# A gated attention and 4-bit FFN block: the order of the rotary step over ScalarE, VectorE and GpSimd

## The reference

```python
def apply_rope(x):
    phase = jnp.tile(pos[:, None] * inv_freq[None, :], (1, 2))[None, :, None, :]
    return (x * jnp.cos(phase) + rotate_half(x) * jnp.sin(phase)).astype(x.dtype)

q = (query @ Wq).reshape(b, t, 32, 128)          # query = layernorm(x)
k = (key @ Wk).reshape(b, t, 8, 128)             # key = value = ctx
v = (value @ Wv).reshape(b, t, 8, 128)
q, k = apply_rope(q), apply_rope(k)
logits = 30 * tanh(einsum(q, k) * 0.0884 / 30)
weights = softmax(where(mask, logits, -1e30))
x = x + tanh(g_xattn) * (einsum(weights, v) @ Wo)
x = x + tanh(g_ffn) * ffn(layernorm(x))          # 4-bit weights, 1376 hidden columns, SiLU
```

## Time and profile before

| what | before |
|---|---|
| median of 3 runs (lowest to highest) | 865.17 us (864.29 to 866.2) |
| the profiled execution, its own time | 864.27 us |
| its span | 862.5 us |
| mean granted TensorE clock in the span | 0.966 |
| PE busy | 774.4 us (90%), 3650 matmuls |
| DVE busy | 641.0 us (74%), 1168 instructions |
| ACT busy | 423.7 us (49%), 823 instructions |
| POOL busy | 602.7 us (70%), 437 instructions |
| chain that ended last, by engine | POOL 51%, PE 25%, issue 15%, DVE 6% |

### The profile page before, as it was taken

How to read it: one execution, slowest core, us unless ns; L and a number is a source line. 1 busy time by engine, 2 the same in 40 slices (tenths; PEclk the granted TensorE clock), 3 DMA queues, 4 the chain that set the end, 5 groups by cost and what they waited for, 6 DMA issues and landing times.

```text
span 862.5 us, 11913 instructions
## 1 busy us (share of the span) xinstructions
PE 774.4 (90%) x3650; PEld 622.0 (72%) x3650; DVE 641.0 (74%) x1168; ACT 423.7 (49%) x823; POOL 602.7 (70%) x437
## 2 busy tenths in 40 slices
PE   4757999999999999999999999999767779999998
PEld 3645777777777777777777777777655557888786
DVE  6338887888888788788878878877776668778531
ACT  2355555555555555555555555554444335555420
POOL 4567787788788778878878887879855446666510
PEclk9878999999999999999999999999887979999999
DMA  8401000300200020020002002110020024443010
GB/s 295 158 0 51 0 25 1 98 1 25 98 1 26 1 98 1 25 98 1 25 1 98 1 25 87 37 44 1 0 59 1 0 61 110 105 101 75 1 62 36
DMA packets 57137, 41.70 MB, mean 48 GB/s; under 512 B 22938, under 2 KB 44442, under 8 KB 57082
## 3 DMA queue, kind: packets, MB, share of 16 engines
q1 hardware_dynamic: 57082, 41.03, 16.2%
HBM read 38.90 MB, written 2.11 MB: 48 GB/s over the span
## 4 chain that ended last, share of the span: by engine, by line
POOL 51%; PE 25%; issue 15%; DVE 6%; ACT 1%; DMA 1%; POOLq 0%; SPq 0%; ACTq 0%; DVEq 0%
POOL aT_lo L559 10%; POOL q_rot L477 9%; POOL q_sin L472 9%; POOL probs L543 8%; POOL wo_lo L463 6%; POOL wq_lo L454 5%; PE bank_q L1146 2%; POOL wkv_lo L459 2%; PE bank_q L1147 2%; PE ps_o L52 2%; PE ps_o L54 2%; PE ps_o L53 2%; PE ps_s L52 1%; PE ps_s L53 1%; PE bank_kv L52 1%
## 5 line engine op out<-in xcount | busy, mean ns | idle before, releaser
L472 POOL TENSOR_TENSOR q_sin<-q_sin,q_tab 128x512 f32<-128x512 f32 x64 | 82.9, 1295 | 112.7 <-ACT q_sin L634 112.7
L52 PE MATMUL bank_q<-xT_hi,wq_hi 128*128 128x512 f32 x256 | 110.0, 430 | 6.2 <-ACT q_sin L634 4.8
L633 ACT COPY q_sin<-bank_q 64x512 f32<-64x512 f32 x64 | 37.3, 583 | 149.7 <-DVE q_cos L847 149.7
L52 PE MATMUL ps_o<-wo_hi,aT_hi 128*128 128x512 f32 x256 | 105.3, 411 | 2.3 <-POOL aT_lo L559 1.6
L54 PE MATMUL bank_q<-xT_hi,wq_lo 128*128 128x512 f32 x256 | 104.4, 408 | 0.0
L53 PE MATMUL bank_q<-xT_lo,wq_hi 128*128 128x512 f32 x256 | 104.1, 407 | 0.0
L559 POOL TENSOR_TENSOR aT_lo<-attn,aT_hi 128x512 fp32r<-128x512 f32 x64 | 101.5, 1586 | 2.4 <-ACT aT_hi L727 2.3
L54 PE MATMUL ps_o<-wo_hi,aT_lo 128*128 128x512 f32 x256 | 102.7, 401 | 0.0
L53 PE MATMUL ps_o<-wo_lo,aT_hi 128*128 128x512 f32 x256 | 102.5, 400 | 0.0
L477 POOL TENSOR_TENSOR q_rot<-q_cos,q_sin 128x512 f32<-128x512 f32 x64 | 83.1, 1299 | 5.0
L997 DVE TENSOR_TENSOR p_lo<-probs,p_hi 128x512 fp32r<-128x512 f32 x54 | 84.2, 1559 | 1.6 <-ACT p_hi L694 1.6
(11 more groups left out here) (231 smaller groups left out, 2256.0 us busy)
## 6 DMA issues: line engine op xcount, KB each, us to landing
wo_raw<-in_Wo SPq DMA_DIRECT2D x8, 1024.0 KB, 5.4
wq_raw<-in_Wq SPq DMA_DIRECT2D x7, 1024.0 KB, 5.6
packed<-in_gate_q SPq DMA_DIRECT2D x40, 64.0 KB, 2.3
packed<-in_up_q SPq DMA_DIRECT2D x40, 64.0 KB, 2.3
packed<-in_down_q SPq DMA_DIRECT2D x10, 256.0 KB, 3.4
acc<-in_x SPq DMA_DIRECT2D x8, 256.0 KB, 5.9
wkv_raw<-in_Wk SPq DMA_DIRECT2D x8, 256.0 KB, 2.8
wkv_raw<-in_Wv SPq DMA_DIRECT2D x8, 256.0 KB, 3.2
```

The costliest lines, as they stand in the source:

```text
L52: nc.tensor.matmul(out, w_hi, m_hi, start=first, stop=False)
L472: nc.gpsimd.tensor_tensor(q_sin[:], q_sin[:], q_tab[:, 1, :].unsqueeze(1).to_broadcast([P, HALF, T]), ALU.mult).then_inc(q_sined, 1)
```

## The change

It changes the rotary step of the q jobs, VectorE's order in a slot, and the order of the opening.

- `turn_q(n)` waits for the bank (`q_done`) rather than for `cos_q(n)`; it stays behind the sum of n-1.
- `cos_q(n)` waits for `turn_q(n)`, multiplies in place in the PSUM bank, and stands behind the rotation of k in the slot.
- The sum moves from GpSimd to VectorE: `add_q(n)` adds the bank and `q_sin` into `q_rot`, behind the scaling of s-2. `make_q(n)` now waits for the sum of n-2, not for its copies.
- VectorE's transposes and row sums of p of s-1 stand behind `add_q` in slot s; before, those of s-2 stood ahead of `cos_q`. They wait for the mask product of s-1.
- In slot 0 ScalarE rounds v ahead of `turn_q(4)`.
- Opening: four banks for the transposes of x rather than two, x2 and x3 loaded ahead of Wq, statistics and powers for four sequences together, four `prep` calls ahead of `make_q(0)`, the mask's transposes behind it, and the other steps reordered.

```diff
-        x_banks = [ps_o[:], ps_pv[:]]
+        x_banks = [ps_o[:], ps_pv[:], ps_x[:], ps_tot[:]]
...
                 load_x(1)
+                load_x(2)
+                load_x(3)
                 for i in range(2):
                     ks = slice(2 * i, 2 * i + 2)
                     sp.dma_start(wq_raw[0][:, ks, :], wq_v[:, ks, 0:GC]).then_inc(ld_wq0[i], 16)
-                load_x(2)
-                load_x(3)
...
-                def rope(n):
+                def sin_q(n):
                     pool.wait_ge(q_turned, n + 1)
...
                     nc.gpsimd.tensor_tensor(q_sin[:], q_sin[:], q_tab[:, 1, :].unsqueeze(1).to_broadcast([P, HALF, T]),
                                             ALU.mult).then_inc(q_sined, 1)
-                    pool.wait_ge(q_sined, n + 1)
-                    pool.wait_ge(q_cosed, n + 1)
-                    wait(pool, qk_split, n - h - AHEAD)
-                    nc.gpsimd.tensor_tensor(q_rot[:, half, h, :, :], q_cos[:], q_sin[:], ALU.add).then_inc(q_roped, 1)
...
                 def turn_q(n):
-                    act.wait_ge(q_cosed, n + 1)
+                    act.wait_ge(q_done, n + 1)
                     wait(act, q_roped, n)
...
-                    if has_q_job(s):
+                    if 0 < s and has_q_job(s):
                         turn_q(s + AHEAD)
                     if runs(s):
                         act.wait_ge(kv_done, s + 1)
                         wait(act, pv_done, s - 3)
                         nc.scalar.copy(v_hi[:, s % 4, :], kv_bank(s)[:, 1, :]).then_inc(v_rounded, 1)
+                    if s == 0:
+                        turn_q(AHEAD)
...
                 def cos_q(n):
-                    dve.wait_ge(q_done, n + 1)
-                    wait(dve, q_roped, n)
-                    nc.vector.tensor_tensor(q_cos[:], q_banks[n % 2], q_tab[:, 0, :].unsqueeze(1).to_broadcast([P, HALF, T]),
+                    dve.wait_ge(q_turned, n + 1)
+                    nc.vector.tensor_tensor(q_banks[n % 2], q_banks[n % 2], q_tab[:, 0, :].unsqueeze(1).to_broadcast([P, HALF, T]),
                                             ALU.mult).then_inc(q_cosed, 1)
+                def add_q(n):
+                    g, half, h = q_job(n)
+                    dve.wait_ge(q_cosed, n + 1)
+                    dve.wait_ge(q_sined, n + 1)
+                    nc.vector.tensor_tensor(q_rot[:, half, h, :, :], q_banks[n % 2], q_sin[:], ALU.add).then_inc(q_roped, 1)
...
-                    if runs(s - 2):
-                        dve.wait_ge(masked, s - 1)
-                        wait(dve, norm_done, s - 2)
-                        nc.vector.transpose(r_tot[:], probs[:, s % 2, :]).then_inc(p_turned, 1)
-                        dve.wait_ge(p_turned, s - 1)
-                        wait(dve, tot_done, s - 2)
-                        nc.vector.reduce_sum(partial[:], r_tot[:].rearrange("p (c e) -> p c e", e=32), AX_X).then_inc(p_summed, 1)
-                    if has_q_job(s):
-                        cos_q(s + AHEAD)
...
                         nc.vector.tensor_tensor(k_rot[:], kv_bank(s)[:, 3, :], k_sin[:], ALU.add).then_inc(k_roped, 1)
+                    if has_q_job(s):
+                        cos_q(s + AHEAD)
...
                         nc.vector.tensor_tensor(attn[:], ps_pv[:], r_tot[:], ALU.mult).then_inc(norm_done, 1)
+                    if has_q_job(s):
+                        add_q(s + AHEAD)
+                    if runs(s - 1):
+                        dve.wait_ge(masked, s)
+                        wait(dve, norm_done, s - 1)
+                        nc.vector.transpose(r_tot[:], probs[:, (s - 1) % 2, :]).then_inc(p_turned, 1)
+                        dve.wait_ge(p_turned, s)
+                        wait(dve, tot_done, s - 1)
+                        nc.vector.reduce_sum(partial[:], r_tot[:].rearrange("p (c e) -> p c e", e=32), AX_X).then_inc(p_summed, 1)
...
-                    wait(pe, q_turned, n - 1)
+                    wait(pe, q_roped, n - 1)
```

More of the change, by code:

```diff
@@ L437, in _, with invert_std @@
                 pool.wait_ge(half_done, 1)
[L439 to L441 removed]
+                def invert_std(half):
+                    bs = slice(half * HALF, (half + 1) * HALF)
+                    pool.wait_ge(var_done, half + 1)
+                    nc.gpsimd.tensor_tensor(rstd[:, bs, :], rstd[:, bs, :], minus_half[:].unsqueeze(1).to_broadcast([P, HALF, 1]),
+                                            ALU.pow).then_inc(rstd_done, 1)
                 def ctx_rest(b):
@@ L464, in split_w, with apply_mask @@
                                                 wo_hi[par][:, part, :].bitcast(F32), ALU.subtract).then_inc(wo_split, 1)
-                def rope(n):
-                    g, half, h = q_job(n)
+                def apply_mask(s):
+                    pool.wait_ge(exp_done, s + 1)
+                    pr = probs[:, s % 2, :].rearrange("p (h t) -> p h t", h=HG)
+                    nc.gpsimd.tensor_tensor(pr, pr, keepT[:].unsqueeze(1).to_broadcast([P, HG, T]),
+                                            ALU.mult).then_inc(masked, 1)
+                def sin_q(n):
                     pool.wait_ge(q_turned, n + 1)
@@ L621, in prep_x @@
                     act.wait_ge(x_T, b + 1)
-                    nc.scalar.copy(xT_hi[:, b, :, :].rearrange("p k t -> p (k t)"), x_banks[b % 2]).then_inc(x_hi, 1)
+                    nc.scalar.copy(xT_hi[:, b, :, :].rearrange("p k t -> p (k t)"), x_banks[b % 4]).then_inc(x_hi, 1)
                 def prep_ctx(b):
@@ L634, in turn_q @@
                     nc.scalar.copy(q_sin[D // 2:D], q_banks[n % 2][0:D // 2]).then_inc(q_turned, 1)
-                for b in range(4):
+                round_w("wq", 0, 0)
+                for b in range(3):
                     prep_x(b)
-                    round_w("wq", 0, b)
+                    round_w("wq", 0, b + 1)
+                prep_x(3)
                 round_w("wkv", 0, 0)
-                prep_x(4)
                 round_w("wkv", 0, 1)
                 prep_ctx(0)
+                prep_x(4)
                 prep_x(5)
@@ L878, in _ @@
                                         ALU.mult).then_inc(tab_done, 1)
-                x_rest(3)
-                norm_moments(4)
                 norm_apply(4)
+                norm_apply(5)
+                dve.wait_ge(tab_done, 2)
+                cos_q(0)
+                x_rest(4)
+                norm_apply(6)
+                x_rest(5)
+                add_q(0)
+                cos_q(1)
+                norm_apply(7)
+                x_rest(6)
+                add_q(1)
+                cos_q(2)
+                x_rest(7)
+                add_q(2)
+                cos_q(3)
+                dve.wait_ge(id_done, 1)
+                nc.vector.reduce_sum(r_tot[:, 0:32], ident[:].rearrange("p (i c) -> p c i", i=4), AX_X).then_inc(fold_done, 1)
                 dve.wait_ge(fold_done, 1)
@@ L884, in _ @@
                                       r_tot[:, 0:32].unsqueeze(1).to_broadcast([P, 4, 32])).then_inc(fold_done, 1)
-                norm_moments(5)
-                norm_apply(5)
-                x_rest(4)
-                dve.wait_ge(tab_done, 2)
-                cos_q(0)
-                norm_moments(6)
-                norm_apply(6)
-                x_rest(5)
-                cos_q(1)
-                norm_moments(7)
-                norm_apply(7)
-                x_rest(6)
-                cos_q(2)
-                x_rest(7)
-                cos_q(3)
+                add_q(3)
                 dve.wait_ge(tg_done, 1)
@@ L1222, in make_kv @@
                     mm.then_inc(kv_done, 1)
-                prep(0)
-                prep(1)
+                for b in range(HALF):
+                    prep(b)
+                make_q(0)
                 pe.wait_ge(mask_step, 6)
@@ L1228, in _ @@
                 nc.tensor.transpose(ps_s[:, 0:T], keep[:], ident[:]).then_inc(keep_T, 1)
-                prep(2)
-                prep(3)
-                for n in range(AHEAD):
-                    make_q(n)
-                    prep(AHEAD + n)
+                prep(4)
+                prep(5)
+                make_q(1)
+                prep(6)
+                make_q(2)
+                prep(7)
+                make_q(3)
                 def slot(s):
```

76 lines of the change are left out of this document (31 added, 45 removed).

## The result

The changed kernel takes 805.25 us (median of 4 runs, 803.22 to 806.05) against 864.73 for the kernel before on the same chip: ratio 0.9307, 95% interval 0.9284 to 0.9329. It is faster by 59.5 us. The forecast was 808.0 in a range of 799 to 827; its sum was 57 us less. The profiled execution took 804.7 us, its span 802.9. Two executions further down stand far out and are left out of every median and ratio: one of run 8's four (1889.38 us) and one of the kernel before that was measured beside runs 8 and 10 (964.59 us, at a granted clock of 0.745).

A forecast was written before the change was run, and what follows sets the result against it. It took a ring of VectorE's list and a ScalarE detour (9.40 us a slot) as the bound, TensorE's 8.68 next. Opening 9, irregular slots 2, steady stretch 37, attention's end 9: 57 less, so 808 us, range 799 to 827.

The forecast's parts named there:

- The ring and the steady stretch: 52 slots: VectorE's list plus a ScalarE detour makes 9.40 us; opened, TensorE sets 8.68, 37 us less.
- the detour of 2.21 us: Each steady slot: from `cos_q` through ScalarE's copies and `v_hi` to `v_lo`, 2.21 us of the 9.40.
- The two small prices: VectorE's list: the moved sum taken at 0.68 us, the in-place product in the bank at no change.
- I take 0.68 for the sum ... VectorE's list is then 9.40 - 1.52 + 0.68 = 8.56: Steady slot: VectorE's list after the change would be 8.56 us, barely below TensorE's 8.68.
- Rival B: Steady slots: VectorE becomes the bound if `qT_lo` meets GpSimd; slots 9.0 to 9.37, 830 to 844 us; chance 0.11.
- Are other rings shorter than 8.68?: Steady slot of the finished change: other dependency loops checked, the mask's longest at 6.9 to 7.7 us, under TensorE's 8.68.
- Three irregular slots: Slots from 53 to 86.78 us: lose their share of 3 x 0.72, 2 us, bounds 0 and 4.
- Opening: Before the first turning of k: shorter q jobs and reordered loads and statistics give 9 us, bounds 4 and 13.
- job 4's release: Opening: job 4 leaves the path to the first k, up to 4.7 us less about 2.1 for castings.
- the point (b): `make_q(n)` now waits for the sum of n-2; with two banks most of a slot hides it.
- Attention's end: Last attention slots: four slots give 2 us and vanished row-sum waits 7, together 9; bounds 3 and 13.
- `p_lo` on GpSimd is late next: Attention's end: one of two reasons to take 7 us, not 9, from TensorE's 9.1 us of row-sum waits.

The follow-up runs named there:

- run 8: Changed kernel with everything ahead of the first slot as before (loads, deviations one by one, two banks, engine order): 824.21 us, ratio 0.9551.
- Run 10: Changed kernel with the feed-forward unpacking in smaller pieces, placed in later slots where VectorE stood idle: 796.56 us, ratio 0.9231.
- Run 1: Changed kernel with the cosine product first again, written to SBUF, and ScalarE's copies waiting for it: 872.85 us, slot 9.89.
- run 6: Changed kernel with one more subtraction like `p_lo` ahead of it on VectorE, into a free buffer: 812.98 us, slot 8.81.
- Run 7: Changed kernel with one more product of constants on GpSimd behind `aT_lo`, in slots up to 55: 816.47 us, slot 8.83.
- Run 2: Kernel before, with only the transpose and row sums moved to the end of the slot before: 884.95 us, slot 9.87.
- Run 9: Kernel before, with only ScalarE's copies first and the cosine product behind the rotation of k, into SBUF: 854.8 us, slot 9.10.
- run 5: Changed kernel with four pieces of feed-forward unpacking moved from the end of slots 56, 59, 61 to behind `kT_lo` of 57, 58, 60, 62: 803.98 us, ratio 0.9288.
- run 4: Changed kernel with the transpose and row sums back in their old place, two slots after the scores: 813.01 us, ratio 0.9402.
- run 12: Run 9 with TensorE waiting for the cosine product, not for the sum, before it fills a bank again: 847.28 us, slot 9.10.
- run 11: Changed kernel with the cosine product written to SBUF, TensorE waiting for the product, not the sum, before refilling the bank: 806.73 us, ratio 0.9351.

## Why the prediction was right, and where it wasn't

**The ring and the steady stretch: right.** Of the sum's 57 us, 37 rest on it, and 36.6 were measured. Run 1 puts the ring back and shows the detour of 2.21 us again; the slot then is 9.89. The two small prices that decided whether VectorE stays below TensorE, the sum at 0.68 and the product in the bank, were right to 0.01.

**Why VectorE stayed below TensorE: by luck of two terms.** The step "I take 0.68 for the sum ... VectorE's list is then 9.40 - 1.52 + 0.68 = 8.56" held `qT_lo` at 0.94 and `p_lo` at 1.56. Measured are 1.56 and 0.68. Rival B's condition, `qT_lo` meeting a GpSimd operation, came true for the most part: with `p_lo` unchanged the list would be 8.56 + 0.62 = 9.18, in B's 9.0 to 9.2. What saved the forecast was the other half of its own sentence, that `p_lo` had 0.9 to give back. The list is 8.18, and run 6 finds about 0.5 of room in it by adding work, so VectorE was 0.5 from being the bound, not 0.12. Run 7 makes it the bound without touching it.

**"Are other rings shorter than 8.68?": yes with all parts in, no with one.** The forecast checked the rings of the finished change only. Run 2 shows a ring that isn't in the list: over cosine product, copies, GpSimd's three operations and the moved row sums, 9.70 while GpSimd still has the sum. Run 9 shows another, through the output addition and the row sums, of 9.1. The copies alone bring the slot to 9.10, either further part to 8.75 or 8.79, both to 8.69. The share of one part depends on which others are in, so the parts' gains don't add up.

**Three irregular slots: 2 forecast, 6.1 measured. Mis-sized.** The step "The next three slots lose their share of 3 x 0.72" took the steady price and left TensorE's clock out. By the earlier trace rows and the row after, TensorE stood idle for 33.78 - 26.78 = 7.0 us before and for 4.95 after, 2.05 less, as forecast; the other 4.0 are in its busy time, 26.78 to 22.76 us for the same matmuls, at a granted clock of 0.81 and of 0.94. No run sets the clock by itself, and a matmul that is slower where TensorE would have waited anyway costs nothing: run 5 has these slots at 0.88 and 27.9 us. So how much of the 4.0 the clock is worth stays open. Run 8 keeps the old opening and has the slots at 29.0, so 4.8 of the 6.1 come without the new opening (clock 0.88); run 4 gives back 3.4 by the place of the row sums alone (clock 0.89, and one wait of 3.9 us for `kT_lo`).

**Opening: 9 forecast, 10.6 measured in this execution.** The first k came between 42.2 and 44.6 us in the runs that share opening and rotation (5, 6, 7, 10), so the gain is 8.4 to 10.8. Its make-up was wrong. I credited the copies-first order with a shorter chain (4.72 down to 3.4 a job) and job 4's release; runs 8 and 9 show that in the old opening this order *costs* 10 us, and run 12 that the cost is TensorE's wait for `q_roped`, the point (b) that I took as hidden. It is hidden in a slot, not in the opening, where jobs follow one another. The new opening's order makes up for it: 21.4 us between run 8 and the changed kernel. Which of its parts does it (four banks, loads, statistics together, `prep` first) no run took apart, and 3.1 of the 10.6 us are again in TensorE's busy time, 27.84 to 24.74 at a clock of 0.90 and 1.00.

**Attention's end: 9 forecast, 5.9 measured. Mis-sized, and "`p_lo` on GpSimd is late next" failed.** The wait for row sums went from 9.1 to 1.4 as forecast. What came late next was `kT_lo`, 8.5 to 15.6 us of waits; I had put "about 1 us later" on the unpacking of one slot, and there are three such slots (56, 59, 61). The step "four times 8.68 is 34.7: 2" failed by it: the four slots take 39.10, 2.4 more than before, and the slots behind them up to the feed-forward stage 8.3 less. In run 4, with the row sums in their old place, slot 57 takes 9.04 and the four 35.11. The unpacking itself was lengthened too: its six operations behind slots 56, 59 and 61 take 9.0 us before, 11.6 in the changed kernel and 5.8 in run 4, where they fall elsewhere against GpSimd's list. Run 10 shows it from the other side: moving only the unpacking takes 9.0 us out of this stage, but only where each piece fits a gap; in run 5 it doesn't.

**Feed-forward stage: right,** 167.5 for 167.8.

Left open: why one slot in eight of run 4 takes 9.17. It is periodic with the weights' pieces, but no run took one of them out.

## What to carry to other kernels

Look for the bound as a ring with a period, not as the longest wait: start-to-start times that add up to the slot show it, and the slack of the next engine caps the gain. After opening one ring, check the next longest in every combination that you might ship; here one of the moves, the row sums, is worth 8 us beside the others (run 4) and cost 20 without them (run 2). Work that must go into a full engine's list goes where that engine waits, in pieces no longer than the wait (runs 5 and 10).

## What the runs showed of the hardware

A VectorE operation with two operands in SBUF is lengthened when GpSimd works at the same time, and GpSimd's with it: `p_lo` 0.68 to 1.32 in run 7 by a GpSimd filler alone, the sum 0.68 to 1.61 in run 11 by taking one operand out of PSUM. The product, the sum and attn's product with one operand in a bank stayed at 0.68 to 0.69 from 100 to 500 us in every run. That is the rule of the Trainium skill (SBUF — State Buffer, "SBUF: two separate sides") that the forecast weighed; the runs agree, with the addition that the cost moves: a given list on GpSimd collides with one rest or the other depending on the phase, and `qT_lo` averaged 0.80, 1.32, 1.57 and 0.78 us in runs 4, 9, the changed kernel and 11. The unpacking's shifts have one operand in SBUF and are lengthened as well: 1.01 us at their shortest, 2.47 at their longest in the changed kernel. No row shows which part of that rule they fall under.
